# Pair stage of a four-layer graph network: field products in two operations per half step with the fields innermost, both one-hots of a batch in one operation

## The reference

```python
src, dst = edge_index                  # dst is sorted
agg = segment_sum(x[src], dst, N)      # sum of the source rows of every node's edges
deg = segment_sum(ones(E), dst, N)
mean = agg / maximum(deg, 1)
h   = relu(mean @ W1n + b1n + x @ W1r + x @ Wl1 + bl1)
out = the same with h, W2n, W2r, Wl2
x   = layernorm(x + out)
```

## Time and profile before

| | |
|---|---|
| median of 3 runs (lowest to highest) | 3864.7 us (3863.82 to 3871.45) |
| span of the profiled execution | 3862.1 us |
| pair stage in it | about 145 to 1345 us |
| busy: PE, PEld | 3026.9 us (78%), 2702.1 us (70%) |
| busy: DVE | 3184.3 us (82%) |
| busy: ACT, POOL | 2167.0 us (56%), 1344.3 us (35%) |

### The profile page before, as it was taken

One profiled execution on the slowest core, in us unless ns is written; L12 is line 12 of the kernel. 1 busy time (PEld: TensorE's weight loads), 2 busy tenths in 40 slices (PEclk: granted clock), 3 DMA queues, 4 the chain that ended last, 5 costly groups with the idle time before them and its releaser, 6 DMA issues.

```text
span 3862.1 us, 125377 instructions
## 1 busy us (share of the span) xinstructions
PE 3026.9 (78%) x50473; PEld 2702.1 (70%) x50473; DVE 3184.3 (82%) x6961; ACT 2167.0 (56%) x5758; POOL 1344.3 (35%) x1644
## 2 busy tenths in 40 slices
PE   0288888888888879999677777777766788778886
PEld 0167777777777669899677777777665777777775
DVE  7599999999999833233699999999986888888896
ACT  5323333333333410001587887887866888888887
POOL 2000000000000000000387787787782555555554
PEclk9999999999999989999899998999986888898887
DMA  8156666666666789898676776777747888888884
GB/s 213 55 165 208 209 208 210 207 207 207 209 209 209 222 315 367 342 330 328 209 252 223 234 247 228 230 250 226 235 157 227 268 259 261 262 275 268 261 264 144
DMA packets 655939, 907.64 MB, mean 235 GB/s; under 512 B 363978, under 2 KB 587883, under 8 KB 636412
## 3 DMA queue, kind: packets, MB, share of 16 engines
q1 hardware_dynamic: 633240, 800.64, 64.5%
q10 hardware_dynamic: 19763, 94.38, 6.5%
q0 software_dynamic: 2352, 4.52, 0.6%
HBM read 651.96 MB, written 247.40 MB: 233 GB/s over the span
## 4 chain that ended last, share of the span: by engine, by line
DVE 37%; PE 29%; DMA 10%; ACT 8%; issue 8%; SPq 2%; POOL 1%; ACTq 0%; DVEq 0%; POOLq 0%
PE ps L630 7%; PE ps L972 7%; DVE U L758 5%; DMA U<-AD 4%; DVE EDG L781 3%; DVE U L1280 3%; DMA T<-ROWS 3%; DVE EDG L1309 3%; DMA A<-ROWS 2%; DVE U L1272 2%; PE ps L1187 2%; DVE U L1659 2%; PE ps L1199 2%; DVE EDG L1664 2%; PE ps L1180 2%
## 5 line engine op out<-in xcount | busy, mean ns | idle before, releaser
L546 ACT ACTIVATE U<-ps 128x512 bf16<-128x512 f32 (+1 forms) x637 | 359.3, 573 | 666.8 <-PE ps L642 666.5
L1157 POOL TENSOR_TENSOR EDG<-U,edge 128x256 f32<-128x256 f32 x343 | 241.6, 705 | 840.2 <-DVE edge L1305 729.4
L1484 ACT ACTIVATE U<-U,T 128x65 f32<-128x65 f32 x1806 | 459.8, 339 | 82.4 <-PE ps L1575 74.0
L1187 PE MATMUL ps<-U 128*128 128x65 bf16 x7203 | 300.0, 198 | 217.2 <-DVE edge L1283 214.9
L491 POOL DMA_INDIRECT U<-REC,nod x49 | 45.0, 918 | 1164.1 <-PE ps L586 1041.8
L972 PE MATMUL ps<-U 128*128 128x192 bf16 x4802 | 418.1, 248 | 31.1 <-DMA U<-AD 30.9
L972 PEld LDWEIGHTS ps<-U 128*128 128x128 bf16 x4802 | 402.8, 98 | 39.9 <-DMA U<-AD 37.0
L1187 PEld LDWEIGHTS ps<-U 128*128 128x128 bf16 x7203 | 261.3, 101 | 239.9 <-DVE edge L1283 236.4
L781 DVE TENSOR_TENSOR EDG<-edge,EDG 128x896 bf16<-128x896 bf16 x686 | 406.6, 618 | 8.9 <-DMA OSD<-EDG 8.0
L1512 POOL TENSOR_TENSOR U<-U 128x455 f32<-128x455 f32 x258 | 275.6, 1068 | 303.4 <-DVE U L1659 303.4
L655 PE MATMUL ps<-EDG,U 128*128 128x193 bf16 x2401 | 311.9, 251 | 62.4 <-ACT U L546 40.9
(11 more groups left out here) (300 smaller groups left out, 7333.9 us busy)
## 6 DMA issues: line engine op xcount, KB each, us to landing
U<-AD SPq DMA_DIRECT2D x98, 1568.0 KB, 8.6
U<-ROWS SPq DMA_DIRECT2D x343, 448.0 KB, 4.4
OND<-EDG SPq DMA_DIRECT2D x343, 224.0 KB, 2.5
OSD<-EDG SPq DMA_DIRECT2D x343, 224.0 KB, 3.2
AD<-U ACTq DMA_DIRECT2D x49, 1568.0 KB, 6.4
EDG<-ROWS SPq DMA_DIRECT2D x343, 224.0 KB, 5.1
U<-OND SPq DMA_DIRECT2D x303, 224.0 KB, 5.3
EDG<-OSD SPq DMA_DIRECT2D x189, 224.0 KB, 4.7
```

The source lines that it names most:

```text
L546: ev4.by(act.activation(prow[i % NPW][:, P * g:P * (g + m)], ps[4 + gg % 2][:, 0:P * m], ACT.Copy))
L1187: ins = pe.matmul(ps[2 + h][:, 65 * k:65 * k + 65], rw[r][:, 2 * P * k:2 * P * k + P], Ws[:, j, s_, 0:65], start=(s_ == 0), stop=(s_ == 2))
L1484: ins = act.activation(V4[k % NV][:, 0, c, :], H[d % 3][:, s, :], ACT.Copy, scale=a4[d % 2][:, s:s + 1])
```

## The change

Four edits, all in the pair stage, here cut to their core:

- The tiles `L_`, `FR` and the bank `ps[3]` (as `psE`) get the field as innermost index (but for k). ACT's copy of the records and PE's slot matmuls address them accordingly.
- `fields` makes all eight products of a chunk at once: five chunks in one operation (n = 1 and 6) and four in a second (n = 3 and 8), where eight operations stood.
- `slots` writes `sdb` in two operations in place of one.
- `OS` and `OD` become halves of one tile `HOT`; one operation per batch makes both, at n = 0 and the odd n.

```diff
-        L_ = [t.bitcast(BF16).rearrange("p (f c k) -> p f c k", f=NF, k=2) for t in (part(o2, 180), part(o2 + 180, 180), EDG[:, 9180:9360])]
+        L_ = [t.bitcast(BF16).rearrange("p (c f k) -> p c f k", f=NF, k=2) for t in (part(o2, 180), part(o2 + 180, 180), EDG[:, 9180:9360])]
...
-        FR = [part(o2 + 3528 * i, 3528).bitcast(BF16).rearrange("p (c f i k) -> p c f i k", c=HC, f=8, k=2) for i in range(2)]
+        FR = [part(o2 + 3528 * i, 3528).bitcast(BF16).rearrange("p (c i f k) -> p c i f k", c=HC, f=8, k=2) for i in range(2)]
...
-        OS = [EDG[:, 4730 + 448 * i:4730 + 448 * i + 448].bitcast(BF16).rearrange("p (c r) -> p c r", r=P) for i in range(NHB)]
-        OD = [EDG[:, 6074 + 448 * i:6074 + 448 * i + 448].bitcast(BF16).rearrange("p (c r) -> p c r", r=P) for i in range(NHB)]
+        HOT = [EDG[:, 4730 + 896 * i:4730 + 896 * i + 896].bitcast(BF16).rearrange("p (s c r) -> p s c r", s=2, r=P) for i in range(NHB)]
+        OS, OD = ([h[:, s, :, :] for h in HOT] for s in range(2))
...
+        psE = ps[3][:, 0:4 * NB].rearrange("p (i f) -> p i f", f=4)
...
-                rec_ev.by(act.activation(L_[j % NL].rearrange("p f c k -> p (f c k)"), psT[:, 0:360], ACT.Copy))
+                rec_ev.by(act.activation(L_[j % NL].rearrange("p c f k -> p f c k"),
+                                         psT[:, 0:360].rearrange("p (f c k) -> p f c k", f=NF, k=2), ACT.Copy))
...
-                        parts = ((0, 4, 0), (4, 6, 2 * NB), (6, 8, 2 * NB))
-                        for f0, f1, o in parts[::-1] if last else parts:
-                            ins = pe.matmul(ps[3][:, o:o + NB * (f1 - f0)], w_, FR[h][:, c, f0:f1, :, k],
+                        parts = ((0, 4), (4, 6), (6, 8))
+                        for f0, f1 in parts[::-1] if last else parts:
+                            ins = pe.matmul(psE[:, :, (2 if f0 else 0):4], w_, FR[h][:, c, :, f0:f1, k],
                                             start=(h + c + k + f0 == 0), stop=(last and f0 == 0))
...
-            def fields(j, h, f0, f1):
-                for f in range(f0, f1):
-                    ins = dve.tensor_tensor(FR[h][:, :, f, :, :], OH[j % 2][:, HC * h:HC * h + HC, :, :],
-                                            bc(L_[j % NL][:, 2 + f, HC * h:HC * h + HC, :].unsqueeze(2), [P, HC, NB, 2]), ALU.mult)
-                    (fld_hot if f == 7 else dv).by(ins)
+            def fields(j, h, c0, c1):
+                n = c1 - c0
+                o_ = OH[j % 2][:, HC * h + c0:HC * h + c1, :, :].rearrange("p c i k -> p (c i) k")
+                l_ = L_[j % NL][:, HC * h + c0:HC * h + c1, 2:NF, :].rearrange("p c f k -> p c (f k)")
+                ins = dve.tensor_tensor(FR[h][:, c0:c1, :, :, :], bc(o_.unsqueeze(2), [P, n * NB, 8, 2]),
+                                        bc(l_.unsqueeze(2), [P, n, NB, 16]), ALU.mult)
+                (fld_hot if c1 == HC else dv).by(ins)
...
-                slot_ev.by(dve.tensor_scalar(sdb[e % 2], bc(ps[3][:, 0:2 * NB].rearrange("p (f j) -> p f j", f=2).unsqueeze(3), [P, 2, NB, 2]),
-                                             -1.0, None, ALU.add))
+                for s in range(2):
+                    ins = dve.tensor_scalar(sdb[e % 2][:, :, s, :, :], bc(psE[:, :, s].rearrange("p (b c) -> p b c", c=7).unsqueeze(3), [P, NH7, 7, 2]),
+                                            -1.0, None, ALU.add)
+                    (slot_ev if s else dv).by(ins)
...
+                hot8.by(dve.tensor_tensor(HOT[r].rearrange("p s c (r k) -> p (s c) r k", k=2), bc(r1v.unsqueeze(1), [P, 14, D, 2]),
+                                          bc(sdb[i % 2][:, b, :, :, :].rearrange("p s c k -> p (s c) k").unsqueeze(2), [P, 14, D, 2]),
+                                          ALU.is_equal))
...
                         elif n in (1, 6):
-                            fields(jb, (1, 6).index(n), 0, 3)
-                        elif n in (2, 7):
-                            fields(jb, (2, 7).index(n), 3, 6)
-                        elif n in (3, 9):
-                            fields(jb, (3, 9).index(n), 6, 8)
+                            fields(jb, (1, 6).index(n), 0, 5)
+                        elif n in (3, 8):
+                            fields(jb, (3, 8).index(n), 5, HC)
...
-                    if i is not None:
-                        hots(i, n)
+                    if i is not None and (n % 2 or n == 0):
+                        hots(i, (n + 1) // 2)
```

More of the change, by code:

```diff
@@ L445, in gnn_kernel @@
         shim = EDG[:, 8940:8958].bitcast(BF16).rearrange("p (c k) -> p c k", k=2)
-        sdb = [EDG[:, 8958 + 98 * i:9056 + 98 * i].bitcast(BF16).rearrange("p (s j k) -> p s j k", s=2, k=2) for i in range(2)]
+        sdb = [EDG[:, 8958 + 98 * i:9056 + 98 * i].bitcast(BF16).rearrange("p (b s c k) -> p b s c k", b=NH7, s=2, k=2) for i in range(2)]
         offb = EDG[0:CP, 9154:9180].bitcast(BF16)[:, 0:NB]
         psT = ps[2][:, 0:256].bitcast(BF16)
+        psE = ps[3][:, 0:4 * NB].rearrange("p (i f) -> p i f", f=4)
         i2v = iota2[:, 2:2 + 2 * NB].rearrange("p (i k) -> p i k", k=2)
@@ L558, in pairs_act @@
                         act.wait_ge(slot_ev.at, e + 1)
-                        slot_ea.by(act.activation(E3[:, e, 2:4, :].rearrange("p f j -> p (f j)"), ps[3][:, 2 * NB:4 * NB], ACT.Copy))
+                        slot_ea.by(act.activation(E3[:, e, 2:4, :], psE[:, :, 2:4].rearrange("p j f -> p f j"), ACT.Copy))
                     if j is not None and n == 0:
@@ L733, in sources @@
                     dve.wait_ge(src_hot.at, j)
-                dv.by(dve.scalar_tensor_tensor(shim, L[:, 1, :, :], float(j), L[:, 0, :, :], ALU.is_equal, ALU.mult))
+                dv.by(dve.scalar_tensor_tensor(shim, L[:, :, 1, :], float(j), L[:, :, 0, :], ALU.is_equal, ALU.mult))
                 own()
@@ L762, in slots @@
             def slots(e):
                 dve.wait_ge(slot_mm.at, 2 * e + 2)
-                dv.by(dve.tensor_scalar(E3[:, e, 0:2, :].rearrange("p f j -> p (f j)"), ps[3][:, 0:2 * NB], -1.0, None, ALU.add))
+                dv.by(dve.tensor_scalar(E3[:, e, 0:2, :], psE[:, :, 0:2].rearrange("p j f -> p f j"), -1.0, None, ALU.add))
                 if e >= 2:
                     dve.wait_ge(hot8.at, NH7 * (e - 1))
-                slot_ev.by(dve.tensor_scalar(sdb[e % 2], bc(ps[3][:, 0:2 * NB].rearrange("p (f j) -> p f j", f=2).unsqueeze(3), [P, 2, NB, 2]),
-                                             -1.0, None, ALU.add))
@@ L770, in hots @@
-            def hots(i, n):
-                b = (n + 1) // 2
+                for s in range(2):
+                    ins = dve.tensor_scalar(sdb[e % 2][:, :, s, :, :], bc(psE[:, :, s].rearrange("p (b c) -> p b c", c=7).unsqueeze(3), [P, NH7, 7, 2]),
+                                            -1.0, None, ALU.add)
+                    (slot_ev if s else dv).by(ins)
+            def hots(i, b):
                 k = NH7 * i + b
                 r = k % NHB
[L774 to L779, removed]
-                for o_, s in ((OS, 0), (OD, 1)) if n == 0 else (((OS, 0),) if n % 2 else ((OD, 1),)):
-                    ins = dve.tensor_tensor(o_[r].rearrange("p c (r k) -> p c r k", k=2), bc(r1v.unsqueeze(1), [P, 7, D, 2]),
-                                            bc(sdb[i % 2][:, s, 7 * b:7 * b + 7, :].unsqueeze(2), [P, 7, D, 2]), ALU.is_equal)
-                    (dv if s == 0 else hot8).by(ins)
@@ new lines, in hots @@
+                dve.wait_ge(slot_ev.at, i + 1)
+                if k >= NHB:
+                    kk = k - NHB
+                    dve.wait_ge(count4.at, NG4 * (kk // NH7) + (7 * (kk % NH7) + 6) // 4 + 1)
+                    dve.wait_ge(hot_st[r].at, 32 * (k // NHB))
+                hot8.by(dve.tensor_tensor(HOT[r].rearrange("p s c (r k) -> p (s c) r k", k=2), bc(r1v.unsqueeze(1), [P, 14, D, 2]),
+                                          bc(sdb[i % 2][:, b, :, :, :].rearrange("p s c k -> p (s c) k").unsqueeze(2), [P, 14, D, 2]),
+                                          ALU.is_equal))
```

## The result

| | before | after |
|---|---|---|
| median (lowest to highest) | 3865.72 us (3863.82 to 3871.45), 4 runs | 4022.34 us (4020.02 to 4025.0), 4 runs |
| ratio, 95% interval | | 1.0396 [1.0382, 1.041] |
| span of the profiled execution, its own time | 3862.1 us | 4021.0 us, 4022.79 us |

The change makes the kernel 4.0% slower. The forecast was 3879 us in a range from 3835 to 3930: the sign was right, the size was far off.

What follows compares the result with a forecast made beforehand. Two loops run side by side, DVE's and PE's; after the change PE's bounds the step. 0.11 (order) plus 0.25 (records) = 0.36 us over 45 steps, +16, less 2, gives +14: median 3864.7 to 3879 us, range 3835 to 3930.

Steps and rivals of the forecast that it cites:

- The two loops: Pair-stage step: DVE's loop from scaling to scaling closes at 23.35 us, PE's through turn, L615 and ranks at 24.07.
- Products and one-hots: DVE, pair stage: merging products saves 0.81 us a step, merging seven one-hots saves 0.48.
- the slots: DVE's `sdb` written in two operations in place of one: 0.07 us added.
- The order: Between ranks and scaling, 1.70 us of product replaces 1.06: +0.64 in PE's loop, 0.11 beyond its slack of 0.53.
- The wait at the sum: DVE's wait for ACT at L801, the sum into `X`: 1.24 us a step in place of 0.62.
- The records: ACT's copy L508, writing runs of two 2-byte elements 40 bytes apart, takes 0.73 us: +0.25 a step.
- pairs are free on ACT: Rival: the record copy costs nothing more, only 0.11 us a step is left, 3868 us; chance 0.22.
- The slot matmuls: PE's L630, 54 in 3.28 us: same columns and loads remain, so nothing added.
- the sign in the prediction's own list: Slot matmuls taking 4.4 us would show the prediction wrong on the slow side.
- runs of two cost double: Rival: PSUM writes in pairs make 98 columns cost 82 ns; +113 us, 3981 with free records; chance 0.08.
- The DVE saving arrives: Rival: PE's stretch from L667 to L615, in its L630 batches, gives up 0.72 us; 3835 us; chance 0.15.
- the rival of 1.3 us: Each element of ACT's record copy L508 pays 4.5 ns: +1.3 us a step, 3929 us; chance 0.15.

Runs made afterwards that it cites:

- experiment 4: All of the change's DVE work, but `FR` and the PSUM bank in the layout of before, so PE's matmuls are those of before; 3865.8 us, ratio 0.9998.
- experiment 6: experiment 4 with the second product of the first half (four chunks) moved ahead of the ranks; 3840.11 us, ratio 0.9924.
- experiment 8: The kernel before, with only the sum into `X` one place later; 3843.56 us, ratio 0.9947.
- experiment 2: The changed kernel with `FR` in three dense groups of fields, three products per half step, PSUM writes still in runs of two; 3973.6 us.
- experiment 9: The changed kernel with one matmul of 392 columns in place of three, remainders summed by a DVE reduction; 3853.09 us, ratio 0.9974.
- experiment 3: experiment 2 with both 98-column matmuls reading two neighbouring fields of the four-field group, next pair 16 bytes on; 4040.57 us.
- run 16: No follow-up run: part of "the next run 16 bytes on", the next pair of neighbouring columns read, 16 bytes further, as in experiment 3.
- run 32: No follow-up run: part of "the next run 32 bytes on", the next group of neighbouring columns read, 32 bytes further, as in the change itself.

## Why the prediction was wrong

Point by point, by its own steps.

- **The two loops** were right, and to 0.02 us. PE's closed at 24.06 with the change's order (experiment 4, forecast 24.07) and DVE's at 23.33 (experiment 6, forecast 23.35). That PE's closed at 23.43 before the change fits experiment 8, where DVE's loop closes at the same figure. That DVE's saving turns into waits was right.
- **Products and one-hots** were right: 2.19, 1.78 and 1.09 us (forecast 2.19, 1.78, 1.08). So were the slots: two L773 take 729.75 - 729.42 = 0.33 us (forecast 0.34).
- **The order**, +0.64 in the PE loop, was right; in experiment 4 it eats the 0.53 of slack and DVE waits 0.60 us at the ranks (forecast about 0.7). The wait at the sum came to 1.01, not 1.24; most of the rest is a new wait of 0.16 us at the one-hot behind the second half's first product.
- **The records** were mis-sized. The term was +0.25 a step; ACT's copy takes 497 ns in place of 472: +0.025, a tenth of it. A run of two 2-byte elements costs almost nothing where a lone one costs 4.5 ns. The rival "pairs are free on ACT" was right in this. The Trainium skill's rule on lines of 16 bytes (SBUF — State Buffer, Specifications, Cachelines), which would have made the pairs free, held here to within those 25 ns.
- **The slot matmuls** are the step that failed: "The same columns and loads remain, so I add nothing." It asked what the new pattern of the writes costs and never what that of the reads does, though the diff changes both in one line. The term is +3.26 us a step, nine times the whole forecast of 0.36. With the reads thus left out, the sign in the prediction's own list, slot matmuls of 4.4 us, was passed at 4.91. On the writes it chose rightly ("I take the first", a run of two costs the same per column): experiment 2 shows it, with 3.24 us a batch. There the Trainium skill's rule (PSUM — Partial Sum Buffer, Specifications), by which any non-contiguous pattern slows matmuls, did not hold.
- **The rival "runs of two cost double"** had a chance of 0.08 and named the wrong operand. It took 98 columns at 82 ns, two cycles a column, and gave 3981 us; the reads cost 93 ns, 2.3 cycles. That its figure comes nearest to the 4022 measured is luck: the writes that it charged are free.
- **"The DVE saving arrives"** failed at the place it named: the batches got dearer. But its reason was sound: one matmul over all fields does give back 3.28 - 3.14 = 0.14 us a batch (experiment 9), 0.28 of the 0.7 us that it allowed itself for both.
- **The range** reached to 3930. With the reads bounded as the records were (nothing, or two cycles for every column that comes in a pair, which is the 113 us that the rival charged to the writes), its upper end would have been 3929 + 113 = 4042. A slip without effect: for the rival of 1.3 us, 0.11 + 1.3 is 1.41 a step and not 1.47, 61 us and not 64.

## What to carry to other kernels

When a layout is changed to suit one engine, list every access that follows it, the reads of each operand and the writes apart, and price each; a single line of a diff may hold two. Here a matmul whose moving operand came in runs of two columns paid about as if every column were read twice, while one longer matmul across the whole group was free, and runs of four, by the count of experiment 3, nearly so. And before counting a saving on the busiest engine, close each loop that ties it to another engine: here 1.2 us a step of less work on DVE was worth nothing in the change's order, 0.63 us once a product was moved out of the stretch in which PE waits (23.96 - 23.33), and 1.28 us once the sum had moved too and PE's batches were shorter.

## What the runs showed of the hardware that was not expected

- TensorE's reads of the moving operand (bf16, columns 4 bytes apart) in runs of two, the next run 16 bytes on: 0.093 us for 98 columns at 2.4 GHz in place of 0.050 (experiment 3). With the next run 32 bytes on the batch costs 4.91 us in place of 4.84, with the 196 columns in runs of four. If the pairs cost the same there, the 196 columns cost 0.087, 0.082 being one column a cycle. Two accesses in 16 bytes were thus not enough for PE, where the rule of the Trainium skill (SBUF — State Buffer, Specifications, Cachelines) asks for no more.
- TensorE's writes to PSUM in aligned runs of two words cost nothing (3.24 us a batch with them and dense reads, experiment 2, against 3.28 before), where every second word alone cost two columns. The matmul of that row, L613, reads columns 4 bytes apart throughout, as the slot matmuls before do, so its reads are not what costs there.
- The duration of a matmul in the profile is not its price. In experiment 3 the 196-column matmuls read densely, and in the batch shown their mean duration is 268 ns, where it was 250. A duration takes in the wait behind the slower neighbour in the pipeline; prices of single matmuls are better taken from batches of known make-up.
- The granted clock of the first batch fell to about 0.57 in 35 of 45 steps of experiment 2, behind an idle time of 1.26 us on PE, and did not in the other ten, behind the same idle time; its cause stays open.
- POOL's gather of the records (L492) shows 2290 ns in place of 915, on an engine that waits most of the time; nothing follows from it for the time. It goes with DVE's products: 915 ns in every kernel with eight products a half step, about 1570 with three (experiments 2 and 3), about 2290 with two, whatever the layout of `FR` and the one-hots. By what mechanism stays open.
